# Gated cross-attention and expert block, one core: context tiles normalised by ScalarE, the output bias added to x by GpSimd, row maxima in two stages, new instruction orders

## The reference

```python
# cross attention: x normalised are the queries; keys and values come from ctx and from x
xn = layernorm(ctx, ln_x_g, ln_x_b)
ln = layernorm(_layernorm(x), ln_l_g, ln_l_b)
q  = ln @ Wq.T
kv = concat([xn @ Wkv.T, ln @ Wlkv.T], axis=1)       # 512 keys
qn, kn = rmsnorm(q) * DH**-0.5, rmsnorm(k)           # 2 heads of 64
attn = softmax(where(mask, qn @ kn.T, -max))
x = x + tanh(g_xattn) * ((attn @ v) @ Wo.T + bo)
# experts: 32 of 64 hidden each, 4 chosen per token
gates = sigmoid(xt @ expert_sel.T); keep the 4 largest
out = (relu(xt @ keys) * gates) @ values             # xt = _layernorm(x)
x = x + tanh(g_ffn) * out
```

## Time and profile before

| | us |
|---|---|
| median of 3 runs | 123.44 (122.72 to 123.64) |
| the profiled execution | 122.81 |
| its span, first to last instruction | 120.7 |
| around the span (122.81 - 120.7) | 2.1 |

### The profile page before, as it was taken

The page is one execution under the profiler, slowest core; times in us unless marked ns, Lnnn a source line. Parts: engine busy times, 40 slices in busy tenths (PEclk is TensorE's granted clock), DMA queues, the critical chain, the costliest instruction groups (busy, mean ns, idle before and its releaser), DMA issues.

```text
span 120.7 us, 2176 instructions
## 1 busy us (share of the span) xinstructions
PE 110.9 (92%) x704; PEld 90.8 (75%) x704; DVE 101.0 (84%) x319; ACT 58.3 (48%) x128; POOL 12.9 (11%) x24
## 2 busy tenths in 40 slices
PE   4999998899979979797999989999999999999990
PEld 4999996488857858476999766676788788888870
DVE  5789969999579899888777869889799889799872
ACT  4957686988991137018452201202555534455421
POOL 6011000800035080800000000000000000000000
PEclk9999999999999999999999999999999999999999
DMA  3799500000000000000001399732819985640004
GB/s 94 209 245 426 214 5 0 0 3 0 0 0 5 0 0 0 0 8 0 0 0 27 125 280 303 227 111 97 249 24 278 304 253 176 203 148 31 0 30 144
DMA packets 6903, 12.74 MB, mean 106 GB/s; under 512 B 813, under 2 KB 2349, under 8 KB 6638
## 3 DMA queue, kind: packets, MB, share of 16 engines
q1 hardware_dynamic: 6894, 12.63, 32.7%
HBM read 11.97 MB, written 0.66 MB: 105 GB/s over the span
## 4 chain that ended last, share of the span: by engine, by line
PE 81%; DVE 7%; ACT 5%; issue 4%; POOL 0%; DVEq 0%; POOLq 0%
PE bank L705 11%; PE bank L707 11%; PE bank L706 11%; PE bank L854 10%; PE bank L714 7%; PE bank L908 6%; PE bank L781 3%; PE bank L808 3%; PE bank L767 3%; PE bank L835 2%; PE bank L735 2%; ACT prob L651 2%; PE bank L841 2%; PE bank L837 2%; PE bank L839 1%
## 5 line engine op out<-in xcount | busy, mean ns | idle before, releaser
L682 ACT ACTIVATE hid_hi<-keys 128x512 fp32r<-128x512 f32 x24 | 15.2, 633 | 18.3 <-PE bank L707 9.2
L528 DVE SCALAR_TENSOR_TENSOR keys<-bank,inT 128x512 f32<-128x512 f32 x32 | 21.2, 684 | 3.2 <-PE bank L707 1.2
L545 DVE TENSOR_TENSOR hid_lo<-keys,hid_hi 128x512 fp32r<-128x512 f32 x24 | 16.0, 685 | 1.1 <-ACT hid_hi L682 1.0
L854 PE MATMUL bank<-vw,prob 128*128 128x129 f32 x128 | 15.8, 278 | 0.2 <-ACT prob L651 0.2
L854 PEld LDWEIGHTS bank<-vw,prob 128*128 128x128 f32 x128 | 14.8, 191 | 0.9 <-issue 0.8
L705 PE MATMUL bank<-xm_hi,k_lo 128*128 128x512 f32 x32 | 14.8, 462 | 0.0
L651 ACT ACTIVATE prob<-bank 128x512 f32<-128x512 f32 x16 | 8.7, 601 | 11.1 <-PE bank L841 11.0
L707 PE MATMUL bank<-xm_hi,k_hi 128*128 128x512 f32 x32 | 12.6, 395 | 0.0
L706 PE MATMUL bank<-xm_lo,k_hi 128*128 128x512 f32 x32 | 12.6, 395 | 0.0
L441 DVE CUSTOM_DVE_ANT_0 junk<-bank,mask_b 128x512 bf16<-128x512 f32 x16 | 10.4, 689 | 1.5 <-PE bank L808 1.5
L714 PE MATMUL bank<-ident 128*128 128x128 f32 x48 | 9.5, 364 | 1.5 <-POOL ident L314 1.5
(11 more groups left out here) (136 smaller groups left out, 228.5 us busy)
## 6 DMA issues: line engine op xcount, KB each, us to landing
inT<-gate_rows SPq DMA_DIRECT2D x32, 256.0 KB, 3.6
keys<-keys_in SPq DMA_DIRECT2D x1, 1024.0 KB, 7.8
values<-values_in SPq DMA_DIRECT2D x1, 1024.0 KB, 9.9
out<-x_mid SPq DMA_DIRECT2D x4, 128.0 KB, 1.7
vecs_x<-x_in SPq DMA_DIRECT2D x1, 256.0 KB, 5.7
wb<-wb_in SPq DMA_DIRECT2D x1, 211.8 KB
wa<-wa_in SPq DMA_DIRECT2D x1, 208.0 KB, 3.1
cx<-ctx_in SPq DMA_DIRECT2D x2, 96.0 KB, 2.6
```

The costliest lines, as they stand in the source:

```text
L528: dve.scalar_tensor_tensor(hid[:, n % 3, :], bank[H_BANK[n % len(H_BANK)]][:, :], 0.0, gated[:, n % SLOTS, :], ALU.max, ALU.mult).then_inc ...
L545: dve.tensor_tensor(hid_lo[:, m % RING, :], hid[:, n % 3, :], hid_hi[:, m % RING, :].bitcast(F32), ALU.subtract).then_inc(hid_lo_ready, 1)
L682: act.activation(hid_hi[:, m % RING, :], hid[:, n % 3, :], ACT.Copy).then_inc(hid_hi_ready, 1)
L854: last = pe.matmul(bank_of(b, OUT + t)[:, WOA * a:WOA * a + WOA], prob[:, b % 2, a, j, P * t:P * t + P], vw[:, b, j, a, :], start=(j == 0) ...
```

## The change

- norm_in: the two context tiles of a batch are normalised by ScalarE (Identity with scale rs and bias nb = -mean*rs); VectorE computes nb in one instruction of 128x2, and no longer touches the tiles. ScalarE's part is a stage norm_in of its own, and turn_in on TensorE waits for both engines.
- The bias leaves the value path. A transfer broadcasts bo to 128 rows, ScalarE scales it by tanh(g_xattn) in the stage constants, and GpSimd writes x_mid0 = x + bo in two instructions of 128x512 (add_bias), behind the low parts of the keys. out_proj waits for them and adds x_mid0 where it added x. The ones row (L590), the products L769 and the 97th row are gone; vlat is one product of 256 columns per tile.
- row_max is two stages per batch, with two products and two reductions each.
- All three tables are new. Among other moves, split_values stand behind weights 3.1 on ScalarE, 6 instead of 16 warm products stand ahead of turn_in 0, and finish 0 stands before the end on VectorE.

```diff
-    row_max 0, vlat 2, vctx 2, turn_max 0, project 2, turn_in 3, weights 0.0, vlat 3, turn_qk 1, vctx 3,
+    row_max 0.0, warm 22, turn_qk 1, warm 23, vlat 2, row_max 0.1, vctx 2, project 2, turn_max 0, vlat 3,
...
+                    sp.dma_start(bo[:, :], wb_in[DH:DH + 1, B_WO:B_WO + D].to_broadcast([P, D])).then_inc(in_bo, 16)
             sp.dma_start(keys[:, :], keys_in).then_inc(in_keys, 16)
...
+            def add_bias(h):
+
+                if h == 0:
+                    pool.wait_ge(bo_ready, 1)
+                    pool.wait_ge(in_x[1], 16)
+                else:
+                    pool.wait_ge(in_x[2], 16)
+                t = slice(HT * h, HT * h + HT)
+                pool.tensor_tensor(x_mid0[:, t, :], x[:, t, :], bo[:, :].unsqueeze(1).to_broadcast([P, HT, D]),
+                                   ALU.add).then_inc(bias_ready, 1)
+
             for b in range(HB):
                 low_parts(b, keys, k_hi, k_lo, keys_hi_ready, keys_lo_ready)
+                add_bias(b)
...
+                dve.scalar_tensor_tensor(nb_in[:, b, :], mv_in[:, b, BT:, 0], -1.0, rs_in[:, b, 3, BT:],
+                                         ALU.mult, ALU.mult).then_inc(nb_ready, 1)
...
-                for t in range(BT):
-                    j = BT * b + t
-                    dve.tensor_scalar(cn[:, j, :], cx[:, j, :], mv_in[:, b, BT + t, 0:1],
-                                      rs_in[:, b, 3, BT + t:BT + t + 1], ALU.subtract, ALU.mult).then_inc(xn_ready, 1)
...
-            def row_max(b):
-                if b == 0:
+            def row_max(b, t):
+                if b == 0 and t == 0:
...
-                for i in range(BT * HEADS):
+                for i in range(HEADS * t, HEADS * t + HEADS):
...
+                if t < BT - 1:
+                    return
...
+                dve.wait_ge(bias_ready, b // HB + 1)
...
-                                                    x[:, j, :], ALU.mult, ALU.add)
+                                                    x_mid0[:, j, :], ALU.mult, ALU.add)
...
+            def norm_in(b):
+                act.wait_ge(nb_ready, b + 1)
+                for t in range(BT):
+                    j = BT * b + t
+                    act.activation(cn[:, j, :], cx[:, j, :], ACT.Identity, bias=nb_in[:, b, t:t + 1],
+                                   scale=rs_in[:, b, 3, BT + t:BT + t + 1]).then_inc(cn_ready, 1)
+
...
-                act.activation(cnT[DC:DC + 1, :, :], ident[DC:DC + 1, 0:1].unsqueeze(2).to_broadcast([1, B, S]), ACT.Exp,
-                               scale=0.0).then_inc(row_ready, 1)
+                act.wait_ge(in_bo, 16)
+                act.activation(bo[:, :], bo[:, :], ACT.Copy, scale=tanh_g[:, 0:1]).then_inc(bo_ready, 1)
...
-                    lat = xnT[:, b, P * t:P * t + P]
-                    for a in range(HEADS):
-                        o = bk[:, D * (HEADS * t + a):D * (HEADS * t + a) + D]
-                        last = pe.matmul(o, lat, folded[:, D * a:D * a + D], start=True, stop=(a > 0))
-                        if a == 0:
-                            pe.matmul(o, wb[:, B_ONE:B_ONE + P], wb[:, B_WO:B_WO + D], start=False, stop=True)
+                    last = pe.matmul(bk[:, HEADS * D * t:HEADS * D * (t + 1)], xnT[:, b, P * t:P * t + P],
+                                     folded[:, 0:HEADS * D], start=True, stop=True)
```

122 lines of the change are left out of this document (61 added, 61 removed).

## The result

The changed kernel takes 118.40 us (median, 117.8 to 120.0) against 123.44 (122.72 to 123.64): a ratio of 0.9585, with an interval of 0.9526 to 0.9644. The forecast was 119.9, in a range of 118.2 to 122.2. The profiled execution took 117.8, so 5.0 less than the profiled one of before. All ratios here leave out executions in which the chip was in a slower state, so a ratio can differ from that of the medians beside it.

The account below looks back on a forecast made before the run. Ahead of the expert part TensorE and VectorE hand work to and fro, neither full; the expert part is TensorE's own. 1.6 removed work plus 2.7 less waiting, less discounts, gives 3.2: 119.9 us predicted, range 118.2 to 122.2.

Parts of the forecast that it names:

- The place and the walk: VectorE's new order ahead of the expert part, followed: first up stage at 65.5 instead of 69.81.
- The sum: Whole kernel: 4.3 us gained ahead of the expert part, less 0.4, 0.2, 0.3 and about 0.2, leaving 3.2.
- case (a): The forecast itself: stretch ahead of the expert part 2.5 to 4.5 us shorter, 118.4 to 121.0 us; chance 0.57.
- the case that I gave 0.04: The rest beside the listed rivals: a gain above 4.5 us; chance 0.04.
- Bo: Start, ScalarE's constants: waiting for the bo transfer costs 0 to 0.7 us, taken as 0.2.
- The clock: Start, TensorE: fewer warm products may delay the rise from 1.2 to 2.4 GHz; 0 to 1.2 us, taken as 0.4.
- VectorE absorbs about half: Start, worst clock case: TensorE 2.4 us late with turn_qk 0, VectorE wants it only at 19.8, so 1.2 lost.
- The work removed: Ahead of the expert part: VectorE net 1.6 us less from context tiles, TensorE 1.8 less from eight bias products.
- TensorE's 7.9 us at row_max: TensorE's 12 waits for VectorE's reductions at row_max, 7.9 us, were to shrink to about one, under 2 as sign.
- Exclusion: GpSimd's v_lo blocks VectorE's refinement steps, 0 to 2.5 us, taken as 0.3; rival: hits of 2.5, 122.0 us, chance 0.09.
- rival d: Split row_max: VectorE's producers hold it elsewhere, only removed work counts, 1.6 - 0.6, 122.1 us; chance 0.10.
- rival e: Expert part: second half's gates come late and TensorE idles, slower, 123.4 us or more; chance 0.05.

Follow-up runs that it names:

- warm_12: The changed kernel with 12 instead of 6 warm products ahead of turn_in 0 on TensorE: 118.28 us, ratio 0.9557 against the kernel before.
- ctx_on_dve: The changed kernel with the two context tiles of each batch normalised on VectorE again, without the nb instruction: 120.15 us, ratio 0.9717 against the kernel before.
- w_ctx_on_dve: The changed kernel with 12 warm products ahead of turn_in 0 and the context tiles back on VectorE: 118.54 us, ratio 0.9579 against the kernel before.
- old_orders: The changed kernel's work under the three order tables of the kernel before, row_max halves back to back: 122.39 us, ratio 0.9944 against the kernel before.
- w_bo_values: The changed kernel with 12 warm products, bo scaled behind project 2, and the values' high parts earlier on ScalarE: 120.47 us, ratio 0.9730 against the kernel before.

## Why the prediction was right, and where its steps were not

**The place and the walk: right, closely.** The walk down VectorE's order put the first up stage at 65.5; it starts at 65.59. It put the maxima of row_max 1 at 33.5 (33.67 by the start and 0.08 of the write), row_max 2.1's at 41.0 (L462 starts at 41.06), row_max 3.1's at 48.9 (48.68), select 1 at 56.9 (56.99, behind a wait of 1.0 as forecast), and its four waits of 0.3, 0.7, 1.0 and 0.7 are there as 0.74, 0.66, 1.00 and 0.68. Up to norm_qk 1 the kernel was some 0.6 ahead of the walk, because the mask on GpSimd ended at 8.87 and not at 9.56 and held nothing; VectorE's longer wait for TensorE, 0.74 instead of 0.3, took most of that back. That the end agrees to 0.1 is partly these two misses cancelling.

**The sum: too small by the discounts.** 4.3 ahead of the expert part was right (4.22), its split less so: VectorE is 2.6 less busy and waits 1.7 less, where the sum had 1.6 and 2.7. Of the extra busy time 0.42 is the hold of the earlier trace rows, which this execution escaped; the rest was not traced. The 1.1 us taken off for clock, bo, exclusion and handovers was not paid in the profiled execution, and the remainder, "the expert part is taken over unchanged", was 0.48 better, with 0.3 more around the span. 4.22 + 0.48 + 0.3 = 5.0, and the gain between the medians is 5.04. By its stretch, 2.5 to 4.5 shorter, this is case (a), and 118.40 is its very edge; by the gain, above 4.5, it is the case that I gave 0.04, which deserved more, since the walk itself said 4.3 gross.

**Bo, 0.2 (0 to 0.7): nothing that can be told.** The transfer landed at 7.96, ScalarE scaled it at 7.98 to 8.38, and moving it away changed 0.9557 to 0.9551.

**The clock, 0.4 (0 to 1.2): the bounds were wrong, the value about right.** In the profiled execution the late rise, near 10.2, cost nothing that can be found: from project 0 to the first score product TensorE takes 12.63 us, and 12.63 in warm_12. But the worst case was put at a rise by 16.4 and 1.2 us. ctx_on_dve showed a rise past 18: the same stretch takes 16.17 (10.23 to 26.40) against 12.81 in w_ctx_on_dve (9.50 to 22.31), 3.4 us more, and from project 0 to the first up product it is still 3.4 (57.19 against 53.83). The step that failed is "VectorE absorbs about half": it absorbs nothing of those 3.4. (The whole difference between the two executions, 122.29 against 118.22, is 4.1; the other 0.7 is a variance write that the mask held, 0.92 at 8.17.) This is one execution of each.

**The work removed: right sum, wrong owner.** The prediction booked 1.6 for VectorE's context tiles and called TensorE's 1.8 hidden in the walk. The runs say 0.3 and 1.6. The reading that failed stands in its first part, "In a row_max TensorE stands behind VectorE": true for row_max, but in the new order its timeline shows no wait on TensorE from 7.33 to 43.12, and from project 1 to the first row_max everything goes through its queue. That the sum came out is partly luck: a change with only the context tiles moved would have been forecast 1.3 too high.

**TensorE's 7.9 us at row_max were read too large.** That view adds the weight-load track and the product track. The waits of TensorE alone, before:

```profile
PE bank L808 <- DVE mx L441: 2.5, 4, 0.8
```

and of the weight loads, before:

```profile
PEld bank L808 <- DVE mx L441: 5.5, 8, 1.1
```

2.5 + 5.5 is the 7.9, of which 2.5 is time without a product. In the changed kernel the same view of the source L827 says

```profile
  DVE mx L455: 0.7, 2
```

all of it on the weight loads. "Under 2 instead of 7.9" was met; the 7.9 was never a possible gain, and the forecast didn't use it as one.

**Exclusion, 0.3 (0 to 2.5): about nothing here, and the rival's price was right.** In the changed kernel one step of norm_mid 3 takes 0.36 at 68.07 while v_lo runs to 68.42: 0.2. Where the orders put them on top of each other it costs 1.8 (old_orders) and 2.2 (w_bo_values), inside the bound of 2.5. The prediction looked only for instructions with two SBUF inputs; the writes of the maxima have one, and were held for 0.86 and 0.99 us more than their 0.18. The Trainium skill ("SBUF — State Buffer", Who interferes with whom) lists copy, cast and tensor_scalar among the instructions that can enter a mode in which they contend with GpSimd. By that rule, old_orders and w_bo_values agree: the writes and the copy end with GpSimd's instruction. It was on the page and I left it out. The prediction also took the hold at the mask as one that the start had always had; in the runs it moves from one small instruction to another and is at times absent.

**Halves of row_max (rival d, 0.10): refuted**, and the other way round more strongly than anyone expected: with this order and the halves together the kernel is slower than before. **Gates of the second half (rival e, 0.05):** the gates of half 1 were written out at 80.83 and read from 84.02, and no up stage of that half waits for them.

What stays open: 0.7 us in the expert part by which the old work is slower under the new orders; which of the many moves in the three tables bring the 2.1% of the orders, since they were run as a whole and only the place of row_max by itself; and whether the 18 warm products behind turn_in 0, which now stand on the pacing engine, could be fewer. That last one was not tried.

## What to carry to other kernels

Walk the new order by hand, engine by engine, from measured stage lengths: it gave the end of the stretch to 0.1 us, and the stages on the way to within 0.6. But charge removed work to the engine that has no wait up to the next meeting point in the *new* order, not to the one that was waited for in the old. And when work goes to GpSimd, look at everything VectorE does in that time, small scalar instructions too: it is their place and not their length that decides, so both engines' orders have to be read together.
